# Joining a soft mixture of experts' combination to the expert loop's block, with early first tiles and written-out gelus

## The reference

```python
E, S, H = (32, 32, 768)             # experts, slots of each and batch, hidden width
xn = _l2norm(x, axis=2)             # x: [b=4, l=512, d=192], layer-normalised before
phin = scale * _l2norm(phi, axis=0)
logits = jnp.einsum('bld,des->bles', xn, phin)
d_w = jax.nn.softmax(logits, axis=-1)
c_w = jax.nn.softmax(logits.reshape(b, l, E * S), axis=-1)
slots = jnp.einsum('bld,bles->besd', xn, d_w)
h = jax.nn.gelu(jnp.einsum('besd,edh->besh', slots, w1) + b1[:, None, :], approximate=False)
eo = jnp.einsum('besh,ehd->besd', h, w2) + b2[:, None, :]
eo = eo.reshape(b, E * S, d)
return jnp.einsum('bkd,blk->bld', eo, c_w)
```

## Time and profile before

| | us |
|---|---|
| Time, median of three runs (lowest, highest) | 1492.51 (1490.99, 1494.38) |
| The profiled execution's own time | 1505.61 |
| Its span, first to last instruction | 1503.8 |
| PE busy in the span | 1314.3 |
| DVE busy | 924.9 |
| ACT busy | 739.7 |
| Expert loop, first matmul to last | 1298.48 to 1449.12 |
| Combination, first matmul to last | 1456.13 to 1499.80 |

### The profile page before, as it was taken

One profiled execution on the slowest core, in us unless ns is written; L12 is line 12 of the kernel. 1 busy time (PEld: TensorE's weight loads), 2 busy tenths in 40 slices (PEclk: granted clock), 3 DMA queues, 4 the chain that ended last, 5 costly groups with the idle time before them and its releaser, 6 DMA issues. The chain is left out here.

```text
span 1503.8 us, 27513 instructions
## 1 busy us (share of the span) xinstructions
PE 1314.3 (87%) x10025; PEld 910.7 (61%) x10025; DVE 924.9 (62%) x2251; ACT 739.7 (49%) x1539; POOL 372.7 (25%) x424
## 2 busy tenths in 40 slices
PE   4779999699569999789999988889858888899988
PEld 3422333346437776567777766777753333699988
DVE  5468886412557777599888879887747866100001
ACT  1326556221124443488888856767643333344433
POOL 6300000000037776456666620000001222100000
PEclk9879999758779999799999999999867999899999
DMA  3342120000133334534344521212005000199931
GB/s 90 91 119 61 47 65 22 24 1 0 31 96 105 93 114 138 154 109 131 103 125 127 146 86 42 70 37 59 1 26 132 1 0 1 50 291 293 299 106 42
DMA packets 113233, 132.61 MB, mean 88 GB/s; under 512 B 27613, under 2 KB 98892, under 8 KB 113020
## 3 DMA queue, kind: packets, MB, share of 16 engines
q1 hardware_dynamic: 111580, 129.48, 30.1%
q0 software_dynamic: 1536, 1.59, 0.4%
HBM read 91.42 MB, written 37.88 MB: 86 GB/s over the span
## 5 line engine op out<-in xcount | busy, mean ns | idle before, releaser
L2283 POOL TENSOR_TENSOR m_cw<-m_E,m_f 128x1024 f32<-128x1024 f32 x16 | 45.1, 2818 | 362.0 <-DVE m_f L2228 362.0
L629 DVE TENSOR_REDUCE mx<-bank 128x1 f32<-128x512 f32 x192 | 119.7, 682 | 18.2 <-PE bank L551 17.8
L689 ACT ACTIVATE PT<-bank 128x1024 f32<-128x1024 f32 x96 | 94.2, 1022 | 68.8 <-PE bank L567 68.0
L1716 POOL TENSOR_SCALAR r_grD<-gr 32x192 f32<-32x192 f32 x192 | 101.8, 530 | 101.9 <-DVE gr L1610 51.6
L2368 DVE TENSOR_TENSOR x_eo<-bank,b 128x192 f32<-128x192 f32 x32 | 11.5, 358 | 153.0 <-PE bank L2345 153.0
L1447 PE MATMUL bank<-r_grD,ek 128*128 128x256 f32 x384 | 100.6, 398 | 0.0
L2356 ACT ACTIVATE x_g<-bank,w 128x128 f32<-128x128 f32 x192 | 53.1, 375 | 85.3 <-PE bank L2334 85.3
L2334 PE MATMUL bank<-slT,w 96*128 x768 | 91.4, 278 | 2.0 <-ACTq L45 2.0
L2334 PEld LDWEIGHTS bank<-slT,w 96*128 96x128 f32 x768 | 90.5, 195 | 2.9 <-issue 2.9
L551 PE MATMUL bank<-K,Q 97*128 97x512 bf16 x192 | 69.9, 416 | 9.0 <-PEq L105 6.2
L1447 PEld LDWEIGHTS bank<-r_grD,ek 128*128 128x128 f32 x384 | 68.2, 191 | 9.4
(11 more groups left out here) (357 smaller groups left out, 3131.2 us busy)
## 6 DMA issues: line engine op xcount, KB each, us to landing
w<-in_m_w SPq DMA_DIRECT2D x32, 579.0 KB, 6.4
w<-in_m_w SPq DMA_DIRECT2D x32, 576.0 KB, 5.8
k_d<-p_krows SPq DMA_DIRECT2D x48, 256.0 KB, 2.8
ek<-k_d SPq DMA_DIRECT2D x32, 384.0 KB
tgt<-c_d SPq DMA_DIRECT2D x33, 196.0 KB
c_d<-p_rows SPq DMA_DIRECT2D x32, 196.0 KB, 2.8
g_d<-gr SPq DMA_DIRECT2D x32, 192.0 KB
o_G<-g_d SPq DMA_DIRECT2D x32, 192.0 KB, 3.0
```

Source lines behind the costliest of these rows:

```text
L629: v.tensor_reduce(mx[u % 2][:, j // 4, j % 4:j % 4 + 1], slot(f"A{u}.{j}"), AX.X, ALU.max).then_inc(*dve.did(f"max{u}.{j}"))
L689: a.activation(PT[kt % 2][:, 2 * hp:2 * hp + 2, :], STB[s % 2][:, :, :], ACT.Exp, scale=DH ** -0.5)\
L1716: last = g_.tensor_scalar(grD[g][rr, :, b, :], b3(gr[j % RING][rr, cols(g)]), 0.0, None, ALU.bypass)
```

## The change

- `moe_combine` and its block are gone. Its PE, DVE and SP work stands in `moe_experts` behind each engine's loop, written out over the 16 tiles. Its sums use banks 6 and 7, which the loop leaves free.
- PE reads the weights from `cT`; the copies on ACT and the buffers `y_c` are gone.
- The first two tiles (`AHEAD = 2`) are summed in two parts: chunks 0 to 6, which only want the moves of turns 0 to 6, and, behind a second wait on `moved`, chunk 7. All other tiles are summed whole after that.
- The last batch's store is split in three: two tiles, one, one.
- ACT's gelus are no longer a hardware loop but a Python loop, so that all 192 instructions stand in a row.

```diff
--- before.py
+++ after.py
@@ -2283,14 +2283,17 @@
                     g.tensor_tensor(e3(cw[n % 2][:, :]), e3(Ed[n % 2][:, :]), bc(f[n % 2][:, :]), ALU.mult).then_inc(*pool.did(f"cw{n}"))
 
 
-def moe_experts(nc, M, ins):
+def moe_experts(nc, M, ins, out):
 
     with ExitStack() as ctx:
         sb = lambda n, s, d=F32: ctx.enter_context(nc.sbuf_tensor(n, s, d))
         sem = lambda n: ctx.enter_context(nc.semaphore(n))
         gT = [sb(f"x_g{i}", [P, HC, P]) for i in range(2)]
         eo = [sb(f"x_eo{r}", [P, D]) for r in range(XE)]
-        ps, ps2, slT, eo_all = M["ps"], M["ps2"], M["slT"], M["eo_all"]
+        h, ps, slT, cT, eo_all = M["h"], M["ps"], M["slT"], M["cT"], M["eo_all"]
+        Y, tiles, AHEAD = [ps[6], ps[7]], range(TILES), 2
+        summed = Steps(sem("x_summed"), [f"y{t}" for t in tiles])
+        added, stored = Steps(sem("x_added"), [f"add{t}" for t in tiles]), sem("x_stored")
         w1, w2, b2, w_in = M["w1"], M["w2"], M["b2"], M["w_in"]
         moved = [sem(f"x_moved{r}") for r in range(XE)]
         R = range(XE)
@@ -2318,8 +2321,15 @@
                         move(sp, q, r)
                 for r in R:
                     move(sp, TURNS - 1, r)
+                for b in range(B):
+                    parts = ((0, TB),) if b + 1 < B else ((0, 2), (2, 1), (3, 1))
+                    for t0, n in parts:
+                        sp.wait_ge(*added.at(f"add{b * TB + t0 + n - 1}"))
+                        sp.dma_start(out[b, t0 * P:(t0 + n) * P, :].rearrange("(t p) d -> p t d", p=P), h[:, b * TB + t0:b * TB + t0 + n, :])\
+                            .then_inc(stored, 16)
                 for r in R:
                     sp.wait_ge(moved[r], 16 * B * TURNS + 1)
+                sp.wait_ge(stored, 16 * (B + 2))
 
             @block.tensor
             def _(t_):
@@ -2346,10 +2356,27 @@
                                                  stop=(c == HC - 1))
                             last.then_inc(*pe.did(f"E{r}"))
 
+                def sum_slots(t, chunks):
+                    for c in chunks:
+                        last = t_.matmul(Y[t % 2][:, 0:D], cT[:, t, c, :], eo_all[:, t // TB, c, :], start=(c == 0), stop=(c == CJ - 1))
+                    return last
+
+                summed.open(t_)
+                for r in R:
+                    t_.wait_ge(moved[r], 16 * B * (CJ - 1) + 1)
+                for t in range(AHEAD):
+                    sum_slots(t, range(CJ - 1))
+                for r in R:
+                    t_.wait_ge(moved[r], 16 * B * CJ + 1)
+                for t in tiles:
+                    if t >= 2:
+                        t_.wait_ge(*added.at(f"add{t - 2}"))
+                    sum_slots(t, range(CJ - 1, CJ) if t < AHEAD else range(CJ)).then_inc(*summed.did(f"y{t}"))
+
             @block.scalar
             def _(a):
                 act.open(a)
-                with a.Fori(0, TURNS) as q:
+                for q in range(TURNS):
                     for r in R:
                         a.wait_ge(*pe.at(f"H{r}", q))
                         for c in range(HC):
@@ -2366,60 +2393,10 @@
                         v.wait_ge(*pe.at(f"E{r}", q))
                         v.wait_ge(moved[r], q * (16 * B) + 1)
                         v.tensor_tensor(eo[r][:, :], ps[4 + r % 2][:, 0:D], b2[r][:, :], ALU.add).then_inc(*dve.did(f"c{r}"))
-
-
-def moe_combine(nc, M, ins, out):
...
+                added.open(v)
+                for t in tiles:
+                    v.wait_ge(*summed.at(f"y{t}"))
+                    v.tensor_tensor(h[:, t, :], h[:, t, :], Y[t % 2][:, 0:D], ALU.add).then_inc(*added.did(f"add{t}"))
 
 
 def soft_experts(nc, M, ins, out):
@@ -2432,8 +2409,7 @@
         M["w_in"] = [ctx.enter_context(nc.semaphore(f"w_in{r}")) for r in range(XE)]
         moe_dispatch(nc, M, ins)
         M["eo_all"] = sb("eo_all", [P, B, CJ, D])
-        moe_experts(nc, M, ins)
-        moe_combine(nc, M, ins, out)
+        moe_experts(nc, M, ins, out)
 
 
 def program(nc, ins, out):
```

## The result

| | kernel before | changed kernel |
|---|---|---|
| Median of 20 runs each, us | 1496.46 (1487.39 to 1509.71) | 1487.70 (1484.39 to 1498.60) |
| Ratio, with 95% interval | | 0.9945 (0.9923 to 0.9967) |
| Profiled execution, span | 1503.8 | 1496.8 |
| Expert loop, first matmul to end of the last | 1298.5 to 1449.1: 150.6 | 1289.6 to 1451.8: 162.2 |
| From there to the span's end (called the tail below) | 54.7 | 45.0 |

The change makes the kernel 0.55% faster, 8.2 us of 1496.46, between 4.9 and 11.5 by the interval; the medians differ by 8.8. The forecast was 9.2 us less and 1483.3 us. The difference is inside the interval. The time is not: 1487.7 lies 0.2 us above the upper end of the range, because 20 runs put the kernel before 4.0 us higher than the three that were known (1496.46 against 1492.51).

The account below looks back on a forecast made before the run. PE was taken to bound the kernel, in the loop and in a serial combination with an idle head and cold clock. PE 8.3 us less, with the tail 9.2; 1492.5 - 9.2 = 1483.3 us, range 1480.5 to 1487.5.

Parts of the forecast that it names:

- The level: Whole kernel: base of 1492.51 us, median of three known runs, from which 9.2 us was taken unscaled.
- its own terms: Bounds: restart +1.1, stall +0.4, landing +0.9 us; other way -0.5 loop, -0.2 and -0.3; plus the three runs' spread.
- The loop is bound by PE alone: Expert loop: PE busy for all 18.60 us of a turn, ACT waiting for it; turn stays 18.60.
- A turn over 18.7 us: Expert loop: one of the signs listed as showing the prediction wrong; a turn was expected to stay 18.60 us.
- The gelus, 0 us: ACT in the loop: seven of eight table loads go, 9.0 us of ACT, all under its wait for PE; gain 0.
- Rival 2: Expert loop: ACT's written-out gelus starve for code under the weight stream; 5.4 us slower, 1497.9 us; chance 0.03.
- The weights in place: Combination: PE reads cT in the same shapes; only the first copy, 1.06 us, was on the path.
- The early tiles and the clock: Behind the loop: 14 matmuls fill 4.55 us at full clock, then a 0.2 us wait and one 0.4 us stall.
- Rivals 1 and 3: Behind the loop: 1, PE waits for code, 1486.8 us, chance 0.08; 3, clock drops at join, 1485.2 us, chance 0.05.
- The last store: Kernel's end: last store 96 KB instead of 384, landing in 2.0 us; 3.15 us against 4.0, gain 0.85.
- The estimate of 2.2 us: Last store: landing time of 96 KB from about 2.0 us fixed plus bytes over 436 GB/s; forecast 0.2 us later.

Follow-up runs that it names:

- the two light ones: Kernel before and changed kernel, each reloading only 192 of 1158 columns of w2 inside the loop: medians 1495.19 and 1484.43 us, ratios 0.9976 and 0.9901.
- store_whole: Changed kernel with the last batch stored as one 384 KB DMA instead of three parts: tail 45.9 us.
- ahead1: Changed kernel with one tile begun early instead of two (AHEAD = 1): tail 46.9 us.

## Why the prediction came out as it did

*The level.* This is the step that failed: "I carry the difference over unscaled: 1492.5 - 9.2". The term 1492.5, the time of the kernel before, was mis-sized: 20 runs measured 1496.46. The three runs were 1490.99 to 1494.38, and the range took their spread for that of a median. In the sets of this case, taken on several chips, the kernel before has medians of 1496.46 (20 runs), 1499.10 (27), 1499.81 (13), 1500.09 (22) and 1507.06 (15), with single runs from 1487.4 to 1514.7. From the first of these the forecast would have been 1496.5 - 9.2 = 1487.3, against 1487.7. The range was also narrower than its own terms: together they reach 1480.8 to 1487.6, and it went to 1487.5. The mechanism and the difference held; of the 4.4 us between 1483.3 and 1487.7, 4.0 are the base. What sets the level of an execution is open, beyond the two sources of scatter named below. The statement that 0.2% can be told from no change was too good: with 20 runs of each kernel the interval reaches 0.22% to either side, with 10 to 12 of the changed one 0.3%.

*"The loop is bound by PE alone".* Right for the execution that was read, and wrong as a property of the kernel. The row itself held the warning: PE busy for 18.60 of 18.60 us, and beside it a DMA share of 1.03 at 293 GB/s. Two engines were full at once. A turn over 18.7 us was named as a sign that the prediction is wrong, and it came: 162.2 us for eight turns are 20.3 for each. It was meant for ACT's code; here it told of late weights. In the fourteen profiles other than the two light ones the loop took 150.6 to 163.7 us. The scatter has a second source, which was not followed: the first attention matmuls (L551) start between 81.9 and 92.5 us in the same profiles, and these 10 us lie ahead of anything that was changed.

*The gelus, 0 us.* Right as far as the runs can tell: ratio 1.001, within 0.997 to 1.005, and waits of the same size with and without. Rival 2, the slower one, is ruled out: ACT never idled for its code in any of the eleven profiles with written-out gelus.

*The weights in place.* Right that the first copy was on the path and that the tiles do not care; worth 1.7 us with its waits, where the copy alone was 1.06.

*The early tiles and the clock.* Right, and closest to the numbers: restart 0.21 us after the 14 matmuls (forecast 0.2), stall 0.4 (0.4), no cold start. From the loop's last matmul to PE's end 1494.25 - 1451.80 = 42.45 us against 42.36 in the sum. Rivals 1 and 3 are out: no code was waited for behind the loop, and the clock stayed at 1.00.

*The last store.* Right in sign, too small: 2.55 us from PE's end to the span's end, not 3.15. The two single-tile stores landed in 1.6 and 1.7, not 2.0, and the rest is shorter issue and closing. The estimate of 2.2 us that the prediction drew from the Trainium skill, DMA: Bandwidth & Descriptors (Two cost components), was the worse of the two, as the 24 KB moves had suggested. The fit that the Trainium skill gives there is for DMAs of the GpSimd path, and these stores are SP's.

Together the tail gave 54.7 - 45.0 = 9.7 us, forecast 9.2. By the experiments: the copy 1.7 (54.7 to 53.0), joining the blocks 0.6 (53.0 to 51.4, less the store's 1.0), the early tiles 6.4 (51.4 to 45.0), the store 1.0. The 0.6 is a sum of unlike parts: PE starts 0.55 us sooner (4.75 us behind the loop instead of 5.30) but takes 0.42 more, as the clock comes back later (44.12 against 43.70), and 0.5 goes behind PE's end, where `store_whole`, with its one large last store, takes 3.5 us to the span's end and the kernel before 4.0.

## What to carry to other kernels

A join of two stages pays by what PE can do while the last results travel: here seven eighths of two tiles filled 4.6 us of a hop through DVE, SP and DMA, and in these executions half of the gain of the first of them was that the clock did not fall. Size such early work by the hop, from the trace. And read a stage's DMA share beside its PE share before calling it bound by one of them: where both are full, its time in a single profile can be the lowest of a scatter, as the 150.6 us were here, and a forecast from a few runs needs a range for the level as wide as that scatter.

## What the runs showed of the hardware that was not expected

The clock answered differently to gaps of nearly the same length. In `ahead1`, PE idled 2.49 us and stayed at 1.00 throughout. In the loop of the changed kernel it idled 2.31 us for weights, and the next 24 records took 4.57 us instead of 2.84. Even in this one loop 1.53 us of idling left the clock alone and 1.61 did not:

```profile
1332.87 2.94 PE L2344 MATMUL bank<-slT,w 96*128 x24 [1.53 <-DMA b<-in_m_b]
...
1354.46 4.57 PE L2344 MATMUL bank<-slT,w 96*128 x24 [2.31 <-DMA b<-in_m_b]
...
1396.15 4.57 PE L2344 MATMUL bank<-slT,w 96*128 x24 [1.61 <-DMA b<-in_m_b]
```

The windows around the gap of 2.31 us:

```profile
1352.00:1354.40 2.40, 0.16 (x2) 0.00 (x0) 0.00 (x0) 1.66 (x6) 0.00 (x0) 1.00 0.93 250
1354.40:1358.90 4.50, 4.44 (x25) 4.45 (x26) 0.00 (x0) 0.00 (x0) 0.00 (x0) 0.62 1.05 273
```

The clock is still 1.00 in the gap; it fell 0.9 us after its end, while PE worked again. So this weight, 2.3 us late, costs 4.0. In the whole loop, 6.3 us of waits went with 5.2 us more of busy time (155.75 against 150.60). What parts the gaps that lose the clock from those that keep it these runs do not say.
